# Biases of the routed experts in one kernel: the down bias as a row of the second weights, the up bias by a product with a table of block owners

## The reference

```python
x = x + layernorm(attention(layernorm(x)))          # 16 heads of 8, causal, rotary
x = x + layernorm(ffn(layernorm(x)))

def ffn(x):                                          # DIM 128, INTER 176, 16 experts, top 2
    scores = softmax(xf @ gate_w + gate_b); top_vals, top_idx = top_k(scores, 2)
    h = einsum('td,edh->teh', xf, w1) + b1
    g = einsum('td,edh->teh', xf, w3) + b3
    a = silu(h) * g
    y = einsum('teh,ehd,te->td', a, w2, cw) + cw @ b2
    z = silu(xf @ sw1 + sb1) * (xf @ sw3 + sb3) @ sw2 + sb2     # shared expert, 352 wide
    return y + z
```

## Time and profile before

| | |
|---|---|
| median of 3 runs | 1472.06 us (1467.08 to 1695.15) |
| the profiled execution, its own time | 1470.54 us |
| span of its trace | 1468.8 us, 27636 instructions |
| granted TensorE clock over the span | 0.922 |
| PE busy / PEld busy | 83% / 48% |
| DVE / ACT / POOL busy | 65% / 49% / 57% |
| first and last up bias (L1557) | 1104.2 and 1399.5 us |

### The profile page before, as it was taken

How to read it: one execution, slowest core, us unless ns; L and a number is a source line. 1 busy time by engine, 2 the same in 40 slices (tenths; PEclk the granted TensorE clock), 3 DMA queues, 4 the chain that set the end, 5 groups by cost and what they waited for, 6 DMA issues and landing times.

```text
span 1468.8 us, 27636 instructions
## 1 busy us (share of the span) xinstructions
PE 1219.1 (83%) x8581; PEld 700.7 (48%) x8581; DVE 954.1 (65%) x2397; ACT 721.2 (49%) x1521; POOL 836.0 (57%) x1047
## 2 busy tenths in 40 slices
PE   1479998989989898899988989988549999999920
PEld 0344554454554554545545455453325555555510
DVE  6388887778778677787777766752324444444467
ACT  0116665656556555565555564645214444444424
POOL 5425556657667476675756645545634555555557
PEclk9759999999999999999999998998668999999965
DMA  2431322321332213322132121431022334333256
GB/s 75 122 95 35 109 76 87 85 79 56 97 91 75 79 56 103 89 70 80 58 108 90 55 77 53 106 96 38 28 68 67 92 99 118 99 94 90 84 157 199
DMA packets 135287, 126.18 MB, mean 86 GB/s; under 512 B 17192, under 2 KB 126186, under 8 KB 130538
## 3 DMA queue, kind: packets, MB, share of 16 engines
q1 hardware_dynamic: 115360, 100.27, 23.9%
q0 software_dynamic: 8704, 18.11, 3.8%
q10 hardware_dynamic: 11082, 6.05, 1.6%
HBM read 78.12 MB, written 45.42 MB: 84 GB/s over the span
## 4 chain that ended last, share of the span: by engine, by line
PE 56%; DVE 17%; POOL 8%; issue 8%; ACT 3%; another core or an unknown queue 2%; DMA 1%; SPq 1%; POOLq 0%; DVEq 0%; ACTq 0%
PE wide L1556 6%; PE wide L1448 6%; DVE mx L1230 6%; PE score L1411 6%; PE heads_ps L1421 5%; PE wide L1538 4%; PE wide L1386 4%; PE score L1399 4%; PE score L1528 3%; POOL values L797 3%; PE wide L1557 2%; PE wide L1450 2%; DVE s_h L1171 2%; PE wide L1479 2%; ACT values L926 2%
## 5 line engine op out<-in xcount | busy, mean ns | idle before, releaser
L926 ACT ACTIVATE values<-score 128x512 f32<-128x512 f32 (+1 forms) x704 | 372.4, 558 | 250.6 <-PE score L1411 228.1
L1230 DVE TENSOR_REDUCE mx<-wide 128x2 f32<-128x1024 f32 (+3 forms) x384 | 390.1, 1038 | 127.7 <-PE wide L1450 113.1
L797 POOL TENSOR_SCALAR_AFFINE_SELECT values<-values 128x512 f32<-128x512 f32 x256 | 170.6, 670 | 321.7 <-ACT values L926 319.6
L1448 PE MATMUL wide<-qk 72*128 72x512 bf16 (+3 forms) x1024 | 248.1, 310 | 18.1 <-DVE mx L1230 15.9
L1411 PE MATMUL score<-qk 75*128 75x512 bf16 (+3 forms) x1024 | 241.1, 306 | 14.4 <-ACT values L926 10.7
L1421 PE MATMUL heads_ps<-values 128*32 128x512 f32 (+3 forms) x2048 | 194.1, 452 | 38.1 <-POOL values L797 37.1
L852 POOL DMA_INDIRECT token_scratch<-spread,e_id x144 | 140.9, 978 | 134.8 <-DVE spread L1275 81.8
L1450 PE MATMUL wide<-maskneg,identb 128*128 128x128 bf16 x1024 | 201.5, 225 | 0.0
L1411 PEld LDWEIGHTS score<-qk 75*128 75x128 bf16 x1024 | 82.5, 98 | 159.3 <-ACT values L926 73.9
L786 POOL DMA_INDIRECT sorted_scratch<-zr,places x128 | 131.7, 1029 | 27.3 <-issue 25.4
L1448 PEld LDWEIGHTS wide<-qk 72*128 72x128 bf16 x1024 | 103.1, 101 | 90.9 <-DVE mx L1230 37.1
(11 more groups left out here) (174 smaller groups left out, 1990.5 us busy)
## 6 DMA issues: line engine op xcount, KB each, us to landing
qk<-parts_scratch SPq DMA_DIRECT2D x192, 192.0 KB
parts_scratch<-spread SPq DMA_DIRECT2D x16, 768.0 KB, 8.4
qk<-sorted_scratch SPq DMA_DIRECT2D x144, 66.0 KB
front<-token_scratch SPq DMA_DIRECT2D x16, 512.0 KB, 4.1
xt<-attn_x SPq DMA_DIRECT2D x16, 256.0 KB, 8.7
xr<-attn_x SPq DMA_DIRECT2D x16, 256.0 KB, 8.9
x_scratch<-z SPq DMA_DIRECT2D x16, 256.0 KB, 4.6
shared_scratch<-s_out SPq DMA_DIRECT2D x16, 256.0 KB, 2.3
```

What stands on the lines that cost most here:

```text
L797: nc.gpsimd.affine_select(out=prob[n][:, :, 0:P], in_=prob[n][:, :, 0:P], compare_op=ALU.is_ge, fill=0.0, base=0, pattern=[[0, HG], [1, P] ...
L926: nc.scalar.activation(free_ap(prob[kb][:, hs_[0], :], [[1, N * len(hs_)]]), score[SCORE_RING.buffer(b, step)][:, 0:N * len(hs_)], ACT.Exp ...
L1230: nc.vector.tensor_reduce(mx[:, h0:h0 + len(hs_), j:j + 1], src, axis=AX.X, op=ALU.max).then_inc(p1_max, 1)
L1448: nc.tensor.matmul(o, q4[e][0:ROWS, h, j * P:(j + 1) * P], k4[e][0:ROWS, h, 0:L], start=True, stop=False)
```

## The change

The down bias is no longer a product of its own. `w2_sb` gets an 89th row in its second half, loaded from b2 by one more DMA, and `e_aT`, now a tile of its own with 96 rows, has rows of ones from partition 64 on written once at the start, of which ACT's copies leave row 88 alone. The second half of `down` multiplies 89 rows.

The up bias stays a product, but its operands change. `bias_rows` now holds all three parts of all 16 experts, 48 rows by 352 columns, at a fixed address. `blk_own`, 48 rows by 144 blocks, is 1 where a row's expert owns the block; it is made once in `tables` by one more matmul (with `prior`) and one more DVE instruction. The stationary operand is one column of it, repeated 128 times. This product now opens the sum, ahead of the float32 product, and the wait for `e_xT_ready` comes behind it.

```diff
-        w2_sb = view(front, F32, [E, 2, P])[0:HALF]
+        w2_sb = view(front, F32, [E, 2, P])[0:HALF + 1]
...
-        upto = sb("upto", [E, E], BF16)
+        upto = sb("upto", [E, NPART, E], BF16)
+        prior = sb("prior", [E, NPART, E], BF16)
-        bias_rows = sb("bias_rows", [NPART, E, WIDE], BF16)
+        bias_rows = sb("bias_rows", [NPART * E, 2 * INTER], BF16)
+        blk_own = sb("blk_own", [NPART * E, NBLK], BF16)
...
-        e_aT = [view(s_h[n], F32, [2, P], INTER)[0:HALF] for n in range(2)]
+        e_aT = [sb(f"e_aT{n}", [3 * P // 4, 2, P]) for n in range(2)]
...
# scalar (batch B - 2)
+                    act.dma_start(w2_sb[HALF:HALF + 1, :, 1, :], b2.rearrange("(o e) d -> o e d", o=1)).then_inc(w2_in, 16)
...
# vector, at the start
+            for n in range(2):
+                nc.vector.memset(e_aT[n][P // 2:3 * P // 4, :, :], 1.0).then_inc(ones_filled, 1)
...
# vector, tables
-                pstep(nc.vector.tensor_copy(last_blk[:], wide[0][0:E, 1, 0:1]))
-                nc.vector.tensor_scalar(past[:], iota_blk[0:E, :], last_blk[:, 0:1], None, ALU.is_ge).then_inc(p_past, 1)
+                pstep(nc.vector.tensor_copy(last_blk[:], wide[0][0:NPART * E, 1, 0:2]))
+                nc.vector.tensor_scalar(past[:], iota_blk[0:NPART * E, :], last_blk[:, 0:1], None, ALU.is_ge).then_inc(p_past, 1)
+                dve.wait_ge(p_past, 1)
+                nc.vector.scalar_tensor_tensor(out=blk_own[:], in0=iota_blk[0:NPART * E, :], scalar=last_blk[:, 1:2], in1=past[:],
+                                               op0=ALU.is_ge, op1=ALU.subtract).then_inc(p_owned, 1)
...
# tensor, tables
-                nc.tensor.matmul(wide[0][0:E, 1, 0:1], upto[:], nblk_b[:], start=True, stop=True).then_inc(p_ends, 1)
+                for o, w in ((wide[0][0:NPART * E, 1, 0:1], upto), (wide[0][0:NPART * E, 1, 1:2], prior)):
+                    last = nc.tensor.matmul(o, w[:].rearrange("s r e -> s (r e)"), nblk_b[:], start=True, stop=True)
+                last.then_inc(p_ends, 1)
...
# tensor, down
-                for half in range(2):
-                    nc.tensor.matmul(o, e_aT[k % 2][:, half, :], w2_sb[:, expert, half, :], start=(half == 0), stop=False)
-                nc.tensor.matmul(o, onesb[0:NPART, :], bias_rows[:, expert, 2 * INTER:], start=False, stop=True).then_inc(e_down, 1)
+                nc.tensor.matmul(o, e_aT[k % 2][0:HALF, 0, :], w2_sb[0:HALF, expert, 0, :], start=True, stop=False)
+                nc.tensor.matmul(o, e_aT[k % 2][0:HALF + 1, 1, :], w2_sb[:, expert, 1, :], start=False, stop=True).then_inc(e_down, 1)
...
# tensor, experts
-                    pe.wait_ge(e_xT_ready, n + 1)
                     if not (isinstance(n, int) and n < 2):
                         pe.wait_ge(e_gated, n - 1)
                     o = wide[k % 2][:, 0, 0:2 * INTER]
-                    nc.tensor.matmul(o, e_xT[k % 2][:], w13_sb[:, of[BG + k], :], start=True, stop=False)
-                    nc.tensor.matmul(o, onesb[0:NPART, :], bias_rows[:, of[BG + k], 0:2 * INTER], start=False, stop=True).then_inc(e_up, 1)
+                    nc.tensor.matmul(o, free_ap(blk_own[:, n:n + 1], [[0, P]]), bias_rows[:], start=True, stop=False)
+                    pe.wait_ge(e_xT_ready, n + 1)
+                    nc.tensor.matmul(o, e_xT[k % 2][:], w13_sb[:, of[BG + k], :], start=False, stop=True).then_inc(e_up, 1)
```

More of the change, by code:

```diff
@@ L430, in program @@
         spare_b = sb("spare_b", [E, P], BF16)
-        last_blk = sb("last_blk", [E, 1])
-        past = sb("past", [E, NBLK], BF16)
+        last_blk = sb("last_blk", [NPART * E, 2])
+        past = sb("past", [NPART * E, NBLK], BF16)
         blk_f = sb("blk_f", [P, NBLK])
@@ L499, in program @@
         p_experts = sem("p_experts")
+        p_owned = sem("p_owned")
+        ones_filled = sem("ones_filled")
         p_done = sem("p_done")
@@ L542, in program @@
         N_FW = 16 * (6 + 2 * NCH)
-        N_IDENT = 10
+        N_IDENT = 11
         GROUPS = NBLK // BG
@@ L701, in _ @@
         def _(pool):
-            for m, s in ((ident, 0.0), (identb, 0.0), (maskneg, 0.0), (before, 1.0), (upto, 1.0), (onesb, 1.0)):
+            for m, s in ((ident, 0.0), (identb, 0.0), (maskneg, 0.0), (before, 1.0), (upto, 1.0), (prior, 1.0), (onesb, 1.0)):
                 nc.gpsimd.memset(m[:], s).then_inc(ident0, 1)
             nc.gpsimd.memset(mhalf[:], -0.5).then_inc(ident0, 1)
-            pool.wait_ge(ident0, 7)
+            pool.wait_ge(ident0, 8)
             nc.gpsimd.iota(blank[:], pattern=[[TOPK * P, 2 * SPARE + ROW]], base=(TS - TOPK * P) * P, channel_multiplier=TOPK,
@@ L725, in _ @@
                                     pattern=[[1, P]], channel_multiplier=-1).then_inc(ident_ready, 1)
-            nc.gpsimd.affine_select(out=upto[:], in_=upto[:], compare_op=ALU.is_ge, fill=0.0, base=0,
-                                    pattern=[[1, E]], channel_multiplier=-1).then_inc(ident_ready, 1)
+            for matrix, compare in ((upto, ALU.is_ge), (prior, ALU.is_gt)):
+                nc.gpsimd.affine_select(out=matrix[:], in_=matrix[:], compare_op=compare, fill=0.0, base=0,
+                                        pattern=[[0, NPART], [1, E]], channel_multiplier=-1).then_inc(ident_ready, 1)
             def inverse_deviation(out_, var, added, before, done, sums=vareps):
@@ L899, in body @@
                     for r in range(NPART):
-                        act.dma_start(bias_rows[r:r + 1, :, :], bias_parts[0:E, r, :]).then_inc(bias_kept, 16)
+                        act.dma_start(bias_rows[r * E:(r + 1) * E, :], bias_parts[0:E, r, 0:2 * INTER]).then_inc(bias_kept, 16)
                         act.dma_start(sb2_rows[r:r + 1, :], bias_parts[E:E + 1, r, 2 * INTER:]).then_inc(bias_kept, 16)
@@ L903, in body @@
                     act.wait_ge(qk_transposed, B)
-                    act.dma_start(w2_sb[:, :, 0, :], w2[:, 0:HALF, :].rearrange("e h d -> h e d")).then_inc(w2_in, 16)
-                    act.dma_start(w2_sb[:, :, 1, :], w2[:, HALF:, :].rearrange("e h d -> h e d")).then_inc(w2_in, 16)
+                    act.dma_start(w2_sb[0:HALF, :, 0, :], w2[:, 0:HALF, :].rearrange("e h d -> h e d")).then_inc(w2_in, 16)
+                    act.dma_start(w2_sb[0:HALF, :, 1, :], w2[:, HALF:, :].rearrange("e h d -> h e d")).then_inc(w2_in, 16)
+                    act.dma_start(w2_sb[HALF:HALF + 1, :, 1, :], b2.rearrange("(o e) d -> o e d", o=1)).then_inc(w2_in, 16)
                 if i == B - 1:
@@ L988, in a_back @@
                     act.wait_ge(e_down, n - 1)
-                nc.scalar.activation(e_aT[k % 2][:], score[k % 2][0:HALF, 0:2 * P].rearrange("p (a b) -> p a b", a=2),
+                nc.scalar.activation(e_aT[k % 2][0:HALF, :, :], score[k % 2][0:HALF, 0:2 * P].rearrange("p (a b) -> p a b", a=2),
                                      ACT.Copy).then_inc(e_aT_ready, 1)
@@ L1351, in tables @@
                 pe.wait_ge(p_blocks, 1)
-                nc.tensor.matmul(wide[0][0:E, 1, 0:1], upto[:], nblk_b[:], start=True, stop=True).then_inc(p_ends, 1)
+                for o, w in ((wide[0][0:NPART * E, 1, 0:1], upto), (wide[0][0:NPART * E, 1, 1:2], prior)):
+                    last = nc.tensor.matmul(o, w[:].rearrange("s r e -> s (r e)"), nblk_b[:], start=True, stop=True)
+                last.then_inc(p_ends, 1)
                 pe.wait_ge(p_past, 1)
-                nc.tensor.matmul(wide[1][:, 0, 0:NBLK], onesb[0:E, :], past[:], start=True, stop=True)
-                nc.tensor.matmul(wide[1][:, 1, 0:NBLK], spare_b[:], past[:], start=True, stop=True).then_inc(p_experts, 1)
+                nc.tensor.matmul(wide[1][:, 0, 0:NBLK], onesb[0:E, :], past[0:E, :], start=True, stop=True)
+                nc.tensor.matmul(wide[1][:, 1, 0:NBLK], spare_b[:], past[0:E, :], start=True, stop=True).then_inc(p_experts, 1)
             def body(i):
@@ L1506, in _ @@
             pe.wait_ge(w13_in, 32)
-            pe.wait_ge(w2_in, 32)
+            pe.wait_ge(w2_in, 48)
+            pe.wait_ge(ones_filled, 2)
+            pe.wait_ge(p_owned, 1)
             def experts_of(g, groups_=1):
```

## The result

The changed kernel takes 1452.6 us (median of 19 runs, 1444.95 to 1465.82), the kernel before 1466.49 us beside it (median of 13 of its 19 runs; six executions near 1690 us, like the 1695.15 of the table above, are left out of it and of every ratio). The ratio is 0.9906, 95% interval 0.9886 to 0.9925: about 14 us gained where I forecast 41, and the time lies above my range, whose upper end was 1446.

A forecast was written before the change was run, and what follows sets the result against it. PE bounds the experts' loop; 0.30 us saved per round over 140 rounds is 42, taken as 41, less 1 lost around the loop: 1470.5 - 41 + 1 = 1430.5 profiled, forecast 1431 us. Range of 8 in 10: 1413 to 1446.

The forecast's parts named there:

- The two steps of the 48-row product: PE's round: switching to 48 rows and back costs a step of about 0.10 us going in and one coming out.
- unknown a: PE's up bias: whether 48 rows make the step; bounds 0 to -0.25 us per round, taken as 0 (steps stay).
- Rival A: No step at 48 rows: PE's round 1.51 us, POOL's floor of 1.66 decides, time 1416 us; chance 0.12.
- The repeated column and the fixed addresses: PE's up bias: repeated-column load costs nothing to 0.05 us, taken as nothing; fewer addresses on PE's queue, 0.
- L1539 removed, 0.31 saved: PE's down sum: dropping the separate bias product saves its two steps, its columns and L1521's exposed load, 0.31 us per round.
- The up bias moved, 0.01: PE's up sum: bias product ahead of the up product takes 1.21 us instead of 1.20, costing 0.01 per round.
- The b2 load on ACT's queue, 0 to 2, taken 0.5: Third load into w2, in front of batch 14's exponentials, costs 0 to 2 us, taken as 0.5.
- The tables, 0.5: Ahead of the loop: longer matmul and copy, new DVE instruction hidden or up to 2 us if POOL holds it; taken 0.5.
- Covers: everything fits, 0.51 to spare: In the loop, DVE's gated value keeps 0.51 us to spare; POOL's border 1.08 late makes silu 0.2 late, which fits.
- Rival B: The next wait takes the place, or PE gives back only 0.16 per round: time 1450, or 1441 to 1448; chance 0.18.
- POOL's floor, 1.66 per block: POOL's own work for a group of blocks takes 6.65 us, 1.66 per block, just under PE's new 1.76.
- The median 1.5 above the profiled time: Whole kernel: the median of the runs was taken to lie 1.5 us above the profiled execution.

The follow-up runs named there:

- rows_96: b2_later with the up bias's two operands padded with zero rows from 48 to 96: 1443.80 us, ratio 0.9804 to the kernel before.
- bias_behind_48: b2_later with POOL's next-group weights worked out before the last scatter, and the 48-row bias product behind the up product: 1438.13 us, ratio 0.9803.
- down_row_only: Changed kernel with b2 loaded one batch later and the up bias as before the change, three rows behind the up product: 1455.78 us, ratio 0.9906.
- b2_later: Changed kernel with the b2 load issued one batch later on ACT's queue, ahead of the w1 and w3 loads: 1443.69 us, ratio 0.9826.
- The 96-row kernels: rows_96 (1443.80 us), and the same kernel with POOL's next-group weights worked out before the last scatter (1425.39 us, ratio 0.9727).

## Why the prediction was wrong in size

The direction and the mechanism held, the sum did not. By its own steps:

- **The two steps of the 48-row product** (unknown a, taken as staying): right, 0.094 in and 0.098 out, by after against rows_96. Rival A named the right counterfactual with 0.25; it is 0.296.
- **The repeated column and the fixed addresses** (taken as 0): right, by bias_behind_48 against down_row_only, 1.755 and 1.753.
- **L1539 removed, 0.31 saved**: right, 2.058 - 1.753 = 0.305.
- **The up bias moved, 0.01**: wrong, 0.065. The term that was mis-sized is the load exposed behind the step. I took 0.05 for 128 columns from the transpose behind L1539 and the same for L1556. The up product's is two loads, one for each pass of the float32 product, and its exposed part is 0.400 - 0.298 = 0.10. The trace of before had a row for it, at the loop's end, which I did not read:

```profile
1400.72 0.71 PE L1538 MATMUL wide<-front,s_h 88*128 x4
1401.36 0.22 PE L1539 MATMUL wide<-bias_rows,onesb 3*128 x1
```

  There a real product stands directly behind a step, and L1539 starts 0.64 after it; in the earlier trace rows these are 0.54. The term came to 0.065 where I had 0.01: 0.055 x 139 = 7.6 us in the loop.
- **The b2 load on ACT's queue, 0 to 2, taken 0.5**: this is the term that was off by most. The issue took 12.30; 7 us of it reach the loop in the traces, and b2_later gains 11.7 in the runs (7 to 17). I priced it by its like, the second load of w2 with 1.91, and took that for the upper bound. But that row was the sign that the queue had begun to hold, since the load ahead of it was short:

```profile
918.77 0.33 ACTq L904 DMA_DIRECT2D front<-ffn_w  x1
```

  A third load behind the same two large ones is not its like.
- **The tables, 0.5**: they cost nothing (2.16 us against 2.59). The new instruction was held for 1.91, near the bound, but the hold moved from one instruction to the other and did not come on top.
- **Covers: everything fits, 0.51 to spare**: nearly. 4.3 us in eight single rounds, two of about 2.6 and one of 3.05. My own list had POOL's border late by 1.08 and DVE's silu by 0.2; it left out the scatter that is held for 2.40, which the trace of before has with 2.79. Rival B happened in small, and with the round only 0.065 shorter (down_row_only) it happened in full: 25.9 us. The cover was thinner than the sum of single steps said, which left out that single waits add up from group to group, and that PE behind a long wait can run at 0.50.
- **POOL's floor, 1.66 per block**: not reached by anything. The 96-row kernels come to 1.75 and 1.84 per round on average, so rival A's 1416 was out of reach even without the step; another wait sets their end, and its cause is open.
- **The median 1.5 above the profiled time**: taken from three runs. The runs beside the result put the median of before at 1466.49, 4.1 below the profiled 1470.54.

Together, for the profiled pair, whose span is 22.5 shorter where my sum had 40: 7.6 for the exposed load, 4.3 for the long rounds and 6.4 for the hold (6.9 less my 0.5), less 1.8 that the first four rounds took less than before (6.95 for 8.72 us). That is 16.5 of the 17.5 us that are missing. The medians of the runs differ by 14 and not by 22.5, because the profiled execution of before lies 4.1 above its median and that of after 4.5 below. In which stage these last 8.6 us lie cannot be read, since only one execution of each kernel has a trace; the hold may cost more in other executions than in the traced one. Part may be that the attention stage differs from run to run: the loop starts between 1098.3 and 1112.0 us in the traces of the kernels without the hold.

That 1452.6 lies next to the 1450 of rival B is luck. B had 0.16 per round gained; it was 0.24, and the hold took the difference.

## What to carry to other kernels

Price a DMA issue added behind large ones on a compute engine's queue by what is in flight on that queue, not by the issue beside it (here 12.30 against 1.91 us), and look how much of it later waits absorb; put small loads ahead of large ones, or where the engine has nothing due. A small product of few rows costs the steps around it and the exposed load behind it: fold it into a product as a row, or pad it to the neighbours' row count. And when one engine is the bound at 100%, look at the order of the engines that follow it too: here the down row alone was worth 14 us or 34 us (ratios 0.9906 and 0.9771), by the place of four instructions on POOL.

## What the runs showed of the hardware

- An 8 KB load was issued over 12.30 us behind two loads of 88 x 16 rows of 512 bytes; ahead of them, all three took 0.55, 0.55 and 2.50 us; a batch later, ahead of the loads of w1 and w3, it took 0.56. The issue ended when 0.96 of the 1.45 MB had moved.
- A bfloat16 product of 96 rows, half of them zeros, is cheaper than one of 48 among products of 88 to 128 rows: 0.094 and 0.098 us less at its sides, and 0.102 less between the passes of the float32 product behind it.
- After a wait of 1.64 us PE ran at granted clock 0.50 for 3.4 us, having been at 1.00; after one of 2.18 us in rows_96 it stayed at 1.00.
- A DVE instruction of 0.29 us was held to 1.91 while POOL worked on other tiles, and of two such in a row only one, in some traces the first (2.02) and in others the second; before, with one, that one was held (2.07). It ended at 1093.09, 0.17 behind a product of POOL's (L782, 1091.65 to 1092.92), and 0.10 to 0.17 behind it in all traces; that it waited for that is not tested by a run.
- POOL held the 114th of its 144 scatters for 2.2 to 3.4 us in all 13 traces, with a packet of the instruction queue in the stretch (after) or with none (b2_later); the cause is open.
